# Storing the relative terms head by head, high and low parts in turn

## The reference

```python
q, k, v = (x @ qkv_w + qkv_b) split into 12 heads of 32
Rh = rel_pos_h[i - j + 47]                        # [48, 48, 32]
Rw = rel_pos_w[i - j + 47]
rel_h = jnp.einsum('bhwc,hkc->bhwk', qr, Rh)      # for each query, 48 numbers by key row
rel_w = jnp.einsum('bhwc,wkc->bhwk', qr, Rw)      # and 48 by key column
bias = (rel_h[..., :, None] + rel_w[..., None, :]).reshape(B * nh, S, S)
attn = jax.nn.softmax(attn + bias, axis=-1)
```

## Time and profile before

| | us |
|---|---|
| median of 3 runs | 2315.34 (2313.85 to 2316.94) |
| profiled execution | 2313.71 |
| its span, first to last instruction | 2312.0 |
| projections of queries, keys, values | 0 to 124 |
| relative terms (`phase_rel`) | 124 to 273 |
| first maxima of attention, before the steady loop | 273 to 330 |

### The profile page before, as it was taken

How to read it: one execution, slowest core, us unless ns; L and a number is a source line. 1 busy time by engine, 2 the same in 40 slices (tenths; PEclk the granted TensorE clock), 3 DMA queues, 4 the chain that set the end, 5 groups by cost and what they waited for, 6 DMA issues and landing times. The chain is left out here.

```text
span 2312.0 us, 34181 instructions
## 1 busy us (share of the span) xinstructions
PE 2063.7 (89%) x11132; PEld 1802.0 (78%) x11132; DVE 1449.1 (63%) x2321; ACT 1500.3 (65%) x2533; POOL 922.1 (40%) x621
## 2 busy tenths in 40 slices
PE   7945279999999999999999999684699999999998
PEld 6922148888888888888888888563588888989997
DVE  5656378999999999999999997376513533020000
ACT  3355228888888888888888888612255555555554
POOL 0051213333333333333333333380445656555553
PEclk9955579999999999999999999877599999999999
DMA  6698764556455564555645653143323534211111
GB/s 208 222 210 214 162 131 81 93 105 127 79 112 98 106 126 80 110 100 106 118 78 109 111 104 98 37 146 117 136 67 104 174 86 130 43 39 30 29 30 16
DMA packets 90710, 247.00 MB, mean 107 GB/s; under 512 B 9209, under 2 KB 43481, under 8 KB 85157
## 3 DMA queue, kind: packets, MB, share of 16 engines
q1 hardware_dynamic: 78912, 223.57, 41.5%
q0 software_dynamic: 10672, 20.46, 5.5%
q10 hardware_dynamic: 960, 0.80, 0.1%
HBM read 179.27 MB, written 65.52 MB: 106 GB/s over the span
## 5 line engine op out<-in xcount | busy, mean ns | idle before, releaser
L895 DVE TENSOR_REDUCE mx<-ps_m 128x1 f32<-128x384 f32 x1212 | 642.0, 552 | 101.7 <-PE ps_m L750 96.3
L607 POOL TENSOR_TENSOR p_lo<-p_f,p_hi 128x768 fp32r<-128x768 f32 x216 | 402.6, 1864 | 713.3 <-ACT p_f L854 713.3
L848 ACT ACTIVATE p_hi<-ps_s 128x768 fp32r<-128x768 f32 x648 | 528.6, 816 | 136.5 <-PE ps_s L764 132.9
L854 ACT ACTIVATE p_f<-ps_s 128x768 f32<-128x768 f32 x648 | 526.1, 812 | 12.3 <-POOL p_lo L607 12.3
L750 PE MATMUL ps_m<-key_hi,query_hi 128*128 128x384 f32 x1240 | 420.1, 345 | 50.3 <-DMA query_hi<-rel_hi_d 39.4
L607 DVE TENSOR_TENSOR p_lo<-p_f,p_hi 128x768 fp32r<-128x768 f32 x432 | 423.5, 980 | 39.7 <-ACT p_f L854 38.6
L761 PE MATMUL ps_s<-query_hi,key_hi 128*128 128x384 f32 x1296 | 338.3, 342 | 10.5 <-DMA query_rest<-m_d 8.5
L774 PE MATMUL ps_o<-p_hi,val 128*65 128x384 f32 x1296 | 331.8, 337 | 5.5 <-POOL p_lo L607 5.4
L764 PE MATMUL ps_s<-query_rest,key_rest 121*128 121x384 f32 x1296 | 331.8, 337 | 0.0
L774 PE MATMUL ps_o<-p_lo,val 128*65 128x384 f32 x1296 | 331.6, 337 | 0.0
L750 PEld LDWEIGHTS ps_m<-key_hi,query_hi 128*128 128x128 f32 x1240 | 232.5, 189 | 95.8 <-DMA query_hi<-rel_hi_d 39.7
(11 more groups left out here) (247 smaller groups left out, 2284.8 us busy)
## 6 DMA issues: line engine op xcount, KB each, us to landing
query_rest<-rel_lo_d SPq DMA_DIRECT2D x36, 864.0 KB
query_rest<-qk_lo_d SPq DMA_DIRECT2D x36, 576.0 KB
query_rest<-qk_hi_d SPq DMA_DIRECT2D x36, 576.0 KB
query_hi<-rel_hi_d SPq DMA_DIRECT2D x12, 864.0 KB, 17.0
w_raw__19801<-w_u SPq DMA_DIRECT2D x12, 768.0 KB, 4.7
w_raw__19802<-w_u SPq DMA_DIRECT2D x12, 768.0 KB, 4.5
w_raw__19803<-w_u SPq DMA_DIRECT2D x12, 768.0 KB, 4.5
w_raw__19804<-w_u SPq DMA_DIRECT2D x12, 768.0 KB, 4.8
```

Of the source, the lines that this page charges most:

```text
L607: engine.tensor_tensor(p_lo[r][:], p_f[idx % 2], p_hi[r][:].bitcast(F32), ALU.subtract).then_inc(lo_done(0, idx)[0], 1)
L848: act.activation(p_hi[r][:], ps_s[:, bank:bank + 2, 0:TB], ACT.Exp).then_inc(hi_ok, 1)
L854: act.activation(p_f[idx % 2], ps_s[:, bank:bank + 2, 0:TB], ACT.Exp).then_inc(f_ok, 1)
L895: dve.tensor_reduce(mx[s // TILES][:, s // 3 % 6, col:col + 1], ps_m[:, c, 0:TB], AX.X, ALU.max).then_inc(mx_ok, 1)
```

## The change

The stores of a half are cut by head, and high and low parts follow each other in turn: eight transfers of 48 partitions and one head each, in place of two with four heads each. The rows' half is stored in two parts, after 12 and after 24 fills, each part with the columns of its fills: eight transfers of half the size, twice. The columns' half is stored whole after its 24 fills. The counts of `r_out` follow (`OUTS`).

The low part of the queries is loaded into partitions 64 to 95 instead of 32 to 63, and GpSimd's copy goes to 32 to 63 instead of 64 to 95. The factor -1 in `neg_lo`, which makes the table's low part, moves with it.

```diff
+        OUTS = (32 * HPT, 64 * HPT)
...
-                    for r, src in enumerate((qk_hi_d, qk_lo_d, qk_hi_d)[0:2]):
+                    for r, src in ((0, qk_hi_d), (2, qk_lo_d)):
                         sp.dma_start(q_sb[g % 2][r * HD:(r + 1) * HD, :, cols].bitcast(F32),
...
             for g in range(GROUPS):
-                for n, a in enumerate(ORDER):
-                    half = FILLS // 2
-                    sp.wait_ge(r_hi, FILLS * g + half * (n + 1))
-                    sp.wait_ge(r_lo, BANKS + FILLS * g + half * (n + 1))
-                    for o, d in ((out_hi, rel_hi_d), (out_lo, rel_lo_d)):
-                        sp.dma_start(d[g * HPT:(g + 1) * HPT, a * SIDE:(a + 1) * SIDE, :].rearrange("h r n -> r h n"),
-                                     o[a].bitcast(F32)).then_inc(r_out[a], 16)
+                for made, a, cols in ((FILLS // 4, 1, slice(0, S // 2)), (FILLS // 2, 1, slice(S // 2, S)), (FILLS, 0, slice(0, S))):
+                    sp.wait_ge(r_hi, FILLS * g + made)
+                    sp.wait_ge(r_lo, BANKS + FILLS * g + made)
+                    for h in range(HPT):
+                        for o, d in ((out_hi, rel_hi_d), (out_lo, rel_lo_d)):
+                            sp.dma_start(d[g * HPT + h, a * SIDE:(a + 1) * SIDE, cols], o[a][:, h, cols].bitcast(F32)).then_inc(r_out[a], 16)
                 if g + 2 < GROUPS:
                     load_q(g + 2)
             for a in range(2):
-                sp.wait_ge(r_out[a], 32 + 32 * GROUPS)
+                sp.wait_ge(r_out[a], OUTS[a] * (1 + GROUPS))
...
-                pool.sem_inc(r_out[a], 32)
+                pool.sem_inc(r_out[a], OUTS[a])
...
-            pool.memset(neg_lo[2 * HD:3 * HD, :], -1.0).then_inc(mask_ok, 1)
+            pool.memset(neg_lo[HD:2 * HD, :], -1.0).then_inc(mask_ok, 1)
...
-                    pool.tensor_copy(q_sb[g % 2][2 * HD:3 * HD, :, cols], q_sb[g % 2][0:HD, :, cols].bitcast(F32)).then_inc(q_twice, 1)
+                    pool.tensor_copy(q_sb[g % 2][HD:2 * HD, :, cols], q_sb[g % 2][0:HD, :, cols].bitcast(F32)).then_inc(q_twice, 1)
...
-                        act.wait_ge(r_out[a], 32 * g + 32)
+                        act.wait_ge(r_out[a], OUTS[a] * (g + 1))
```

## The result

The kernel after takes 2289.68 us, the median of 4 runs (2287.38 to 2291.07); the kernel before, timed beside it, 2315.31 (2313.85 to 2316.94). The ratio is 0.9891, with a 95% interval of 0.9876 to 0.9906: 25.6 us faster, where 16 were forecast. The profiled execution took 2290.41 us, its span is 2288.7.

What follows compares the result with a forecast made beforehand. The stage of `phase_rel` was taken as bound by its stores. With pairs at 17 us, 11.0 us of VectorE's stall and 5.0 at the end go, 16.0 in all: 2299 us beside the median 2315.34, range 2281 to 2313.

Steps and rivals of the forecast that it cites:

- The bound and the mechanism: Relative-terms stage: bound by stores read from one partition set after the other; turns by head let engines read both.
- X: Time of a pair of high and low stores (3.54 MB) on the DMA engines; forecast to fall from 22 to 17 us.
- the lower bound: Least time allowed for a pair of stores: 10.8 us, 3.54 MB at the mixed stretch's 327 GB/s.
- The sum: Forecast start times through the stage, half by half, putting attention's first load at 257.1 instead of 273.07: 16.0 us off.
- the first rival: High and low stores still serialize, a pair staying at 20 to 22 us: 0 to 2.4 us gained, about 2314; chance 0.16.
- Issue at nothing: SP's store issues, 72 instead of 12: eight take 3 us beside 17 of transfer, nothing on the path.
- the second rival: Each SP issue has its own price, 2.7 us: 36 us slower, 2351; signs: issues strung out, engines idle between; chance 0.07.
- The early part at nothing: Rows' half in two parts: first part ready 6 us earlier, but engines busy with query loads; 0, bounds 0 and 6.
- The queries' move at nothing: Low queries to partitions 64 to 95: first pair could start 0 to 4 us sooner; taken as 0, same turn kept.
- Serialized transfers: Engines reach high and low at the same time, a pair staying at 20 to 22 us; about 2314; chance 0.16.
- SP as the bound: Store issues on SP's queue cost 2.7 us each, sixteen per rows' half taking 43 us; 36 us slower, 2351; chance 0.07.
- Full overlap: Both partition sets read at once, a pair taking 12.8 us: 31 us off, 2284 (2278 at 10.8); chance 0.15.

Runs made afterwards that it cites:

- run 1: Kernel after, with low stores reading the high part's rows (partitions 0 to 47), so stored low terms are wrong; whole execution 2329.16 us, stage 155.3 us.
- run 2: Kernel after, with the same small transfers but four high ones first, then four low ones, in each eight; 2312.63 us, ratio 0.9986.
- run 8: Kernel after, with high and low parts stored by one transfer of 112 partitions per head, 17% more bytes; 2284.04 us, ratio 0.9857.
- run 5: Kernel before, with one edit alone: stores cut by head, high and low in turn; 2289.25 us, ratio 0.9891.
- run 3: Kernel after, with the rows' half stored whole after its 24 fills, by head in turn; 2292.77 us, ratio 0.9904.
- run 4: Kernel after, with the low queries back in partitions 32 to 63, factor and GpSimd's copy moved back too; 2293.47 us, ratio 0.9895.
- run 6: Kernel after, with group 2's query loads issued ahead of group 0's columns' stores instead of behind them; 2293.6 us, ratio 0.9903.
- run 10: Kernel after, with eight useless HBM-to-HBM copies of queries (2.36 MB) issued ten fills before the last columns' pair is ready; 2289.08 us, ratio 0.9895.
- run 7: Kernel after, with the last columns' pair issued from two queues, high parts by SP and low parts by GpSimd; 2295.3 us, ratio 0.9913.

## Why the prediction was right, and where its sizes were not

**The bound and the mechanism** held as far as the runs reach. The stage was bound by its stores, their time hung on the partitions that they read and on the order (runs 1, 2 and 8), and the order by head was the edit that counted (runs 2 and 5). That some engines read one set while others read the other is inferred: no view shows what an engine reads at a time. It was faster, as forecast, and 2289.68 lies in the range of 2281 to 2313.

**The size of X** is the term that was off. The forecast took 17 us for every pair, the old rate without its tail. Two values stand in its place. From a standing start a columns' pair takes 14.3: the last one's packets run from 232.0 to about 246.3, at 252 GB/s; the rate itself rose from 207, not only the tail went. For rows' halves behind query loads X is 8.6 (3.54 MB at 413), below even the 10.8 that was the lower bound, because that bound came from the 327 GB/s of a mixed stretch. The trace of before showed 408 GB/s only for loads, and I took it for no bound of a store.

**The sum**, term by term, against measured starts: rows of group 1 at 168.0 by forecast and 162.03 measured, with no stall at all; columns of group 1 at 185.3 and 179.56; rows of group 2 at 202.8 and 198.12; columns of group 2 at 221.6 and 214.14; attention's first load at 257.1 and 248.01. The first step is off by 6.0 (4.4 of a stall that the forecast kept and that didn't come, 1.6 by which the fills came earlier) and the last by 9.1, so two thirds of the error stood after the first rows' half. Of the stall 16.9 us went, not 11.0; at the end 6.7, not 5.0. The end gained less than X did (7.7 from 22), because 1.7 us instead of 0.7 lay between the last packets and attention's load.

One reading behind the sum was off before any run. 22 us is the time of the last pair, which stands alone. The pairs ahead of it overlapped, and ScalarE's waits for them ended 20.1, 22.8 (with query loads) and 19.0 us after one another; the first and the last of these four rows of the kernel before, beside the two in the earlier trace rows:

```profile
169.88 9.14 ACT L506 CAST out_both<-ps 48x384 fp32r<-48x384 f32 x24 [8.68 <-DMA rel_lo_d<-out_both]
...
231.75 15.59 ACT L506 CAST room<-ps 48x384 fp32r<-48x384 f32 x24 [9.88 <-DMA rel_lo_d<-room]
```

With X = 22 throughout, the sum's own steps put attention's first load at about 280.6 and not at 273.07; they give no gain at an X near 20.5. So 17 was a fall of 5 us for the last pair and of 2 to 3 for those ahead, and the first rival's X of 20 to 22 is worth its 2.4 us only at 20.

**Issue at nothing** was right for its effect, not for its look. Issues of a columns' half did string out, at 1.4 to 2.2 us, half of the sign that the forecast gave for the second rival. The other half, engines idle between them, didn't come: their busy share is 0.89 to 0.92 in those stretches. And before, where a pair had two issues in all, it took longer. Both fit issues that wait for transfers under way, not transfers that wait for issues.

**The early part at nothing** was right (run 3, and run 5). **The queries' move at nothing** was right within its bounds of 0 to 4: the loads went from 203 to 229 GB/s, and the first fills gained about 0.5 us (run 4). The reason given, that the same turn would be taken, was wrong, since the rate did rise.

**The rivals.** Serialized transfers fell: the last pair's rate rose from 207 GB/s with a tail to 252 without. The 6% of the Trainium skill (SBUF — State Buffer, "Can I just issue two DMAs to hit both halves?"), by which X would be 20.7, doesn't agree with this trace, where X is 14.3. SP as the bound fell: sixteen issues of a rows' half cost nothing on the path. Full overlap, at 2284, came true and more for the halves behind loads (8.6 us against its 12.8), and not for the others; the time lies between it and the forecast. From attention's first load on all was shifted: TensorE's first matmul comes 9.9 us behind it (10.8 before).

## What to carry to other kernels

When a set of transfers touches partitions in two separate places, look at whether all engines are in one place at a time: a tail of half-busy engines and a rate near that of few partitions are the signs. Taking turns in the order of issue gave 25 us here for no change in work; one transfer that spans both places gave 5 more, though it moved 17% more bytes. When a diff holds three edits, try each alone: two of these did nothing that the time shows.

## What was not expected of the hardware

- Stores issued while query loads were under way passed at 406 to 415 GB/s, those of 48 partitions without loads ahead at 252 to 274 (the kernel after, runs 3 and 6); HBM-to-HBM copies ahead of them had no such effect (run 10), and two stores of four heads each kept a high rate for some 4 us only (the kernel before, 315 GB/s).
- Two queues for one pair, high parts in one and low parts in the other, were slower than one: 18.9 us against 16.8, in one profiled execution of each (run 7).
- An issue on SP mostly takes 0.3 to 0.6 us while loads are under way, and mostly 1.3 to 2.8 from the third on while stores of columns are (runs 1 and 6). What it waits for there stays open.
